# A graph layer with a mixer and experts on one core: TensorE signals by drains, a ring of 16, one ScalarE scaling instead of two, and norm weights folded ahead

## The reference, cut to what matters

```
xn = layernorm(x)
hconv(x, W, b):  xt = x @ W
                 m   = segment_sum(xt[src], dst) / (edges of the dst)
                 out = segment_sum(m[dst], src) / (edges of the src)
                 return out + b
h = prelu(hconv(xn, W1, b1), a);  h = prelu(hconv(h, W2, b2) + xn, a)
x = x + h + mix(xn)          # linear attention: k, v normed per head, dots = sum k v, out = q dots / n
x = x + ffn(layernorm(x))    # its own norm, gamma, beta; top 2 of 8 experts, 256 -> 512 -> 256, gelu
```

## Time and profile before

| | |
|---|---|
| median of 3 runs | 8475.15 us (8469.13 to 8481.79) |
| the profiled execution | 8563.98 us, its span 8562.2 us |
| mean granted TensorE clock in it | 0.743 of full speed |
| PE, DVE, POOL, ACT busy | 55%, 44%, 48%, 16% |

### The profile page before, as it was taken

The page is one execution under the profiler, slowest core; times in us unless marked ns, Lnnn a source line. Parts: engine busy times, 40 slices in busy tenths (PEclk is TensorE's granted clock), DMA queues, the critical chain, the costliest instruction groups (busy, mean ns, idle before and its releaser), DMA issues. The chain is left out here.

```text
span 8562.2 us, 93336 instructions
## 1 busy us (share of the span) xinstructions
PE 4688.6 (55%) x16858; PEld 2911.1 (34%) x16859; DVE 3784.0 (44%) x11251; ACT 1385.0 (16%) x4213; POOL 4105.5 (48%) x4256
## 2 busy tenths in 40 slices
PE   3116976666666645555554455445444544454796
PEld 1014533333333323333332233333223322334564
DVE  5105754444444444444444444444433433367323
ACT  0004843333333300000000000000000000000242
POOL 4761034444444445555555465566565556532342
PEclk7558988888788767787776677777666666666898
DMA  2002011222222142222223333333532222231114
GB/s 85 0 21 72 0 43 58 59 59 59 59 59 59 57 103 78 77 81 80 79 76 76 102 107 108 108 108 110 121 121 83 82 82 83 83 74 51 33 62 130
DMA packets 330997, 639.22 MB, mean 75 GB/s; under 512 B 81808, under 2 KB 201444, under 8 KB 330448
## 3 DMA queue, kind: packets, MB, share of 16 engines
q0 software_dynamic: 191808, 490.67, 21.1%
q1 hardware_dynamic: 131396, 140.16, 5.0%
q10 hardware_dynamic: 7756, 7.97, 0.3%
HBM read 551.49 MB, written 87.01 MB: 75 GB/s over the span
## 5 line engine op out<-in xcount | busy, mean ns | idle before, releaser
L525 POOL DMA_INDIRECT gbuf<-table,idxb x3520 | 3354.6, 953 | 3058.3 <-ACT idxb L650 1351.3
L1342 PE MATMUL PS<-gbuf,ohg 128*128 128x257 f32 x7040 | 2549.8, 494 | 2923.0 <-DVE acc L940 1543.0
L1342 PEld LDWEIGHTS PS<-gbuf,ohg 128*128 128x128 f32 x7040 | 1572.3, 242 | 3818.4 <-DVE acc L940 2000.4
L940 DVE TENSOR_TENSOR acc<-acc,PS 128x257 f32 x3520 | 1498.0, 426 | 2999.0 <-remote 1290.7
L949 DVE TENSOR_SCALAR ohg<-iota,dl 128x128 f32<-128x128 f16 x2664 | 796.0, 305 | 519.9 <-issue 499.9
L1311 PE MATMUL PS<-region 128*128 128x440 f16 x3328 | 851.6, 383 | 0.0
L650 ACT COPY idxb<-idx 128x4 int32 (+1 forms) x884 | 168.0, 190 | 3690.7 <-DVE acc L940 2775.5
L640 ACT ACTIVATE region<-region,acc 128x128 f16<-128x128 f16 x838 | 336.4, 401 | 1300.4 <-DVE region L891 1139.6
L1311 PEld LDWEIGHTS PS<-region 128*128 128x128 f16 x3328 | 355.3, 107 | 337.7 <-issue 100.5
L534 POOL DMA_INDIRECT scattered_d<-acc x384 | 370.2, 964 | 142.7 <-issue 120.2
L890 DVE TENSOR_SCALAR region<-iota_c,acc 128x880 f16<-128x880 f16 x838 | 394.4, 471 | 53.1 <-issue 53.1
(11 more groups left out here) (282 smaller groups left out, 3791.9 us busy)
## 6 DMA issues: line engine op xcount, KB each, us to landing
gbuf<-table,idxb POOLq DMA_INDIRECT x3520
table<-acc SPq DMA_DIRECT2D x21, 896.0 KB, 6.7
region<-xt_d SPq DMA_DIRECT2D x98, 128.0 KB
gbuf<-ye_d SPq DMA_DIRECT2D x12, 1024.0 KB, 7.8
xpad_d<-acc SPq DMA_DIRECT2D x1, 6272.0 KB, 21.8
xn_d<-acc SPq DMA_DIRECT2D x49, 128.0 KB
xt_d<-acc SPq DMA_DIRECT2D x49, 128.0 KB
table<-acc SPq DMA_DIRECT2D x49, 128.0 KB
```

Source lines behind the costliest of these rows:

```text
L525: gp.indirect_dma_start(gbuf[:, k, 0:F], None, tables[p], bass.IndirectOffsetOnAxis(idxb[:, k:k + 1], 0)).then_inc(s_g[k], 16)
L940: TT(a, a, PS[:, 4 + k % AB, 0:FC], ALU.add).then_inc(s_acc[p], 1)
L1342: m = MM(PS[:, 4 + k % AB, 0:FC], ohg[:, k, :], gbuf[:, k, :], start=True, stop=True)
```

## The change

- **Signals.** PE's increments in both histograms (now after every second block), in both ranks, in sort 0 (`s_used`, each fourth column) and in all four passes (`s_mm`) come after a drain. Passes 0 and 1 keep groups of two chunks and four banks; passes 2 and 3 signal after four chunks, use eight half banks and products 256 wide. In pass 0 the two sort columns of a group stand behind its signal; in the other passes `body` stands before the signal.
- **Rank 1 and first norm.** The loop is written out. One drain in each block covers its transposes, its rank matmuls and the product of the block before; SP and ACT wait on finer semaphores, and SP's settling is gone.
- **Sorts.** RING is 16, LEAD (how far the blocks' numbers are read ahead) 8. `ohs` is gone: DVE's compare multiplies by field 1 plus 1 and writes `ohv` directly, and ACT scales that once by (field 2 part) / (field 1 plus 1). For this `fields` gets a reciprocal and a product over 832 columns, and `unpack` a subtraction.
- **Leaky unit of pass 1.** Seven fused operations of 256 columns for a group of seven blocks (times the inverse count, plus bias), ACT makes the negative and the positive part, and one fused operation joins them.
- **Prelude of the experts.** Gamma and beta are folded into W1, Wr, b1 and br during turns 16 to 24 of pass 3. The second norm follows from the variance of the first; POOL's `scale_shift` is gone, ACT normalizes, loads are double.

```
-    AB = 4
-    GP = 2
-    RING = 8
+    RING = 16
+    def banked(p):
+        return 4 if p < 2 else 8
+    def group(p):
+        return 2 if p < 2 else 4
...
-        TS(ohs[o][:, k % RING, :], iota_h[:, :], slot_of[o][:, ds(c, 1)], None, ALU.is_equal).then_inc(s_oh[o], 1)
+        TS(ohv[:, k % RING, 0, :], iota_h[:, :], slot_of[o][:, ds(c, 1)], field_a[o][:, ds(c, 1)],
+           ALU.is_equal, ALU.mult).then_inc(s_oh[o], 1)
...
-        A(ohv[:, k % RING, 0, :], ohs[o][:, k % RING, :], ACT.Copy, scale=field_a[o][:, ds(c, 1)])
-        A(ohv[:, k % RING, 1, :], ohs[o][:, k % RING, :], ACT.Copy, scale=field_b[o][:, ds(c, 1)]).then_inc(s_ohs[o], 1)
+        A(ohv[:, k % RING, 1, :], ohv[:, k % RING, 0, :], ACT.Copy, scale=field_b[o][:, ds(c, 1)]).then_inc(s_ohs[o], 1)
...
-                m.then_inc(s_hist, 1)
+                if b % 2 or b == NB - 1:
+                    signal(s_hist)
...
                 if o == 0 and k % SG == SG - 1:
-                    m.then_inc(s_used, 1)
+                    signal(s_used)
...
-                        if k % GP == 0:
-                            pe.wait_ge(s_acc[p], i * U + (U + k + GP - AB))
-                        m = MM(PS[:, 4 + k % AB, 0:FC], ohg[:, k, :], gbuf[:, k, :], start=True, stop=True)
-                        if k % GP == GP - 1:
-                            m.then_inc(s_mm[p], 1)
+                        if k % group(p) == 0:
+                            pe.wait_ge(s_acc[p], i * U + (U + k + group(p) - banked(p)))
+                        MM(chunk_sum(p, k), ohg[:, k, :], gbuf[:, k, 0:width(p)], start=True, stop=True)
                         if body is not None:
                             body(i, k)
+                        if k % group(p) == group(p) - 1:
+                            signal(s_mm[p])
+                            if columns:
+                                for c in range(k + 1 - group(p), k + 1):
+                                    sort_column(1, i, c)
...
+                link(V.reciprocal(pos, field_a[o][:, 0:EC]))
+                link(TT(field_b[o][:, 0:EC], field_b[o][:, 0:EC], pos, ALU.mult))
...
+                link(TS(a, a, 1, 0, ALU.subtract, ALU.max))
...
+            def fold_body(i, k):
+                if k == 4:
+                    pe.wait_ge(s_shift, i - FOLD + 3)
+                    for kt in range(KT):
+                        m = MM(PS[:, 0, :], fa_["shift"][:, kt, :], fr["w1"][:, ds(i - FOLD, 1), kt, :].rearrange("p a h -> p (a h)"),
+                               start=kt == 0, stop=kt == KT - 1)
+                    signal(s_fold)
...
-                link(norm(lambda j: accs[1][:, ds(q * G + j, 1), 0:F].rearrange("p a f -> p (a f)"), lambda j: low[:, j, :], s_v1, s_d1, q, n))
-                norm(lambda j: low[:, j, :], lambda j: low[:, j, :], s_v2, s_d2, q, n).then_inc(s_xh, 1)
```

More of the change, by code:

```diff
@@ L92, in gps_layer @@
     G = 4
+    FOLD = 16
     ER = 4
@@ L548, in _ @@
                 pool.wait_ge(s_sc[h], SC_TURNS * U * 16)
-            pool.wait_ge(s_lnfree, NR7 + 1)
+            for n in range(3):
+                pool.wait_ge(s_lnd[n], NR7 * PART[n] * 48)
             pool.wait_ge(s_wd, 32)
@@ L703, in _, with fold_gamma @@
             idx_pass(2, 0, TURNS)
-            idx_pass(3, 0, TURNS)
+            def fold_gamma(i, k):
+                if k == 12:
+                    act.wait_ge(s_fold, i - FOLD + 2)
+                    settle(act)
+                    for kt in range(KT):
+                        w = fr["w1"][:, ds(i - FOLD, 1), kt, :].rearrange("p a h -> p (a h)")
+                        A(w, w, ACT.Copy, scale=fr["gb"][:, 0, kt:kt + 1])
+            idx_pass(3, 0, FOLD)
+            act.wait_ge(s_fold, 1)
+            for kt in range(KT):
+                A(fr["wr"][:, kt, :], fr["wr"][:, kt, :], ACT.Copy, scale=fr["gb"][:, 0, kt:kt + 1])
+            idx_pass(3, FOLD, FOLD + NE, fold_gamma)
+            idx_pass(3, FOLD + NE, TURNS)
             def act_first(q, par, n):
@@ L1053, in _, with fold_beta @@
             dve.wait_ge(s_zero, 5)
-            acc_pass(3, 0, TURNS)
+            def fold_beta(i, k):
+                if k == 8:
+                    dve.wait_ge(s_fold, i - FOLD + 2)
+                    b = fa_["b1r"][:, ds(i - FOLD, 1), :].rearrange("p a h -> p (a h)")
+                    TT(b, b, PS[:, 0, :], ALU.add).then_inc(s_shift, 1)
+            acc_pass(3, 0, FOLD)
+            dve.wait_ge(s_fw, N_FW)
+            for kt in range(KT):
+                m = TS(fa_["shift"][:, kt, :], ones[:, :], fr["gb"][:, 1, kt:kt + 1], None, ALU.mult)
+            m.then_inc(s_shift, 1)
+            TS(sm["nega"], a_col[:, 0:1], -1.0, None, ALU.mult).then_inc(s_shift, 1)
+            dve.wait_ge(s_fold, 1)
+            TT(fr["br"], fr["br"], PS[:, 1, 0:NE], ALU.add).then_inc(s_shift, 1)
+            acc_pass(3, FOLD, FOLD + NE, fold_beta)
+            acc_pass(3, FOLD + NE, TURNS)
             dve.wait_ge(s_acc[3], NC + U)
@@ L1265, in _ @@
                 rank(0, b)
+                signal(s_rank)
             pe.wait_ge(s_put, NB)
@@ L1327, in _, with product_pass @@
             close_sort(0)
-            def product_pass(p, start, end, body=None):
+            def product_pass(p, start, end, body=None, columns=False):
                 if start == 0:
@@ L1448, in pe_third @@
                 m.then_inc(s_lg, 1)
-            by_group(pe, pe_first, pe_second, pe_third)
+            for q in range(2):
+                turn_sums(q, G)
+                second_weights(q, q, G)
+            for q in range(1, NG - 1):
+                turn_sums(q + 1, G)
+                turn_rows(q - 1, (q - 1) % 2, G)
+                second_weights(q + 1, (q + 1) % 2, G)
+                logits(q - 1, G)
+            turn_sums(NG, 1)
+            turn_rows(NG - 2, 0, G)
+            second_weights(NG, 0, 1)
+            logits(NG - 2, G)
+            turn_rows(NG - 1, 1, G)
+            logits(NG - 1, G)
+            turn_rows(NG, 0, 1)
+            logits(NG, 1)
             pe.wait_ge(s_ecnt, 1)
```

303 lines of the change are left out of this document (165 added, 138 removed).

## The result

The changed kernel takes 8732.67 us (median of 4 runs, 8730.18 to 8759.25) where the kernel before takes 8478.47 (4 runs, 8469.13 to 8496.68): ratio 1.030, 95% interval 1.028 to 1.033. It is slower by 254 us. I had forecast 123 us: the direction was right and the time lies within the range, but the loss is twice the one that I forecast.

The account below looks back on a forecast made before the run. No single bound: no engine is busy for more than 55% of the span. Terms -3 + 52 + 97 + 92 + 0 - 30 - 100 + 15 = +123 us, added to 8475.15, gave 8598 us, 1.4% slower; range 8320 to 8780.

Parts of the forecast that it names:

- the drains of pass 0 ahead of the hole: Pass 0: half of 8 drains a turn fall where PE waits anyway for late signals, so they cost nothing.
- the prelude: Prelude of the experts: DVE bounds it and sheds statistics, normalizations and other work, -100 us, bounds -70 and -120.
- pass 0: Pass 0: four of 8 drains a turn cost PE 0.47 us each over 52 turns, +97 us, bounds 0 to +195.
- the head: Before sort 0: fields, unpack and histogram 0 cost time, rank 1 gains 24 us; together -3, bounds -60 and +40.
- the leaky unit: Leaky unit of pass 1: a group goes from 9.17 to 4.9 us, seven times, -30 us, bounds -15 and -35.
- sort 0: Sort 0: 112 drains at 0.47 us each, since PE has no gap there, +52 us, bounds 0 and +70.
- pass 1: Pass 1: four of 8 drains a turn cost 0.47 us each over 49 turns, +92 us, bounds 0 and +245.
- passes 2 and 3: Passes 2 and 3: drain costs equal the gains from fewer DVE waits and more banks, 0 us, bounds -165 and +198.
- The rival that signals come sooner: Passes: drains bring DVE's adds into the hole if lateness belongs to increments on matmuls; about 8071 us, chance 0.14.
- moves no number: Sort 0 and pass 0: ACT's fused scaling does nothing; already part of the forecast at 0 us, no chance of its own.
- a signal does miss its place as in the rival: Pass 1: a delayed signal misses the hole, +5 instead of +1.9 us a turn, 8750 us, chance 0.12.
- clock: Sort 0: short gaps from drains halve PE's clock, +334 us, 8930 us, chance 0.04.

Follow-up runs that it names:

- The copy first: The changed kernel with ACT's copy of the previous group's transposed rows moved ahead of its work on the next group in the prelude: 8687.13 us, ratio 1.027.

## Why the prediction was right in direction and wrong in size

Two terms failed: the drains of pass 0 ahead of the hole, put at nothing, and the prelude, put at -100 us. The medians lie 131 us above the forecast. By the table's stages, the prelude is 62 us off, pass 0 30, the head 15, the leaky unit 4, sort 0 2, pass 1 -60, and passes 2 and 3 -12. The remaining 88 or so are in the two profiles' places about their medians.

- **"Each turn thus has a hole for the late signals of PE"**: right, and the drains were late as the rows of the old ones said. The rival that signals come sooner is out: DVE's waits only changed their name, and POOL's waits for row numbers in pass 0 did not get shorter (834 us before, 956 after).
- **Sort 0**: right, +52 forecast, +54 measured.
- **Pass 0, the step that failed**: "Half of them, by the pattern of the earlier trace rows, lie in the rush and half ahead of the hole, where PE waits anyway: 4 × 0.47 = 1.9 us". The drains ahead of the hole were costed at nothing, since PE waits there anyhow. But it waited, in most turns, only after it had used its free banks up to chunk 9; a drain makes it stop at the first late completion. The run without drains prices this: 3.5 us a turn for the stops where I had 0, and 1.3 for the four drains of the rush where I had 1.9, together 4.7 to 4.8 us a turn and 246 us over the pass, above the upper bound of 195 that I had given. In the kernel before the same drains cost 136 us, with the 86 us above open. The stage grew by 127 where +97 was forecast. That it comes that near is partly luck: without its drains the changed kernel needs 113 us less than before (1873 against 1986, the latter from the long profile), a term that I had put at 0 ("hidden", "moves no number"), and with its drains nothing of that is left.
- **Pass 1**: +92 forecast, +32 measured, 17 of it by the drains in the changed kernel; in the kernel before they cost 54. The hole now comes before chunk 4 in 48 turns, where it came before chunk 6 in 46, so a signal does miss its place as in the rival, but the turn grows by 0.5 us and not by 5. That PE has slack behind its hole there is my reading and not tried.
- **Passes 2 and 3**: 0 forecast, and 15 for the fold; +3 measured. Two terms lie under it: the drains cost 52 us, and something else gives them back, which was not separated.
- **Leaky unit**: right, -26 where -30 was forecast; the timeline after has 4.8 us a group where 4.9 was forecast.
- **Prelude, mis-sized**: -100 forecast, -38 measured. "DVE is busy for 217 of 272 us, and bounds it" held only before the change. With DVE's work down from 217 to 129 us the limit became ACT's order, which holds back the logits. The copy first gave 59 of the missing 62 us.
- **Head**: -3 forecast, +12: rank 1 ended 6 us later, since histogram 0 took 6 us more and the scatter ended 13 us later, and fields 1 took 6 us more.
- **"A difference of 100 us taken from it is wrong by about 1 us"**: wrong. It treats the 88.8 us by which the profiled execution lay above the runs as a scale factor. The kernel before spreads by as much: its runs beside the later kernels on late chips took 8435 to 8561 us. If these us lie in the passes, as the kernel before with drains makes likely, the passes together grew by up to 250 us where I had summed 204 with the fold.
- The **clock** did not halve in sort 0: granted at 0.99 over 390 us, with gaps of 0.21 us behind each 16 matmuls, as this timeline of PE in the changed kernel shows. The Trainium skill (TensorE: Matmul & The Clock Gate, "A second HAM failure mode: psum-queue depth-cycling") warns of such short idles; this stage does not bear it out.

```profile
801.52 3.14 PE L1368 MATMUL PS<-acc,region 128*128 128x440 f16 x16 [0.21 <-issue]
804.88 3.14 PE L1368 MATMUL PS<-acc,region 128*128 128x440 f16 x16 [0.21 <-issue]
```

## What to carry to other kernels

A drain is not free where its engine is about to wait: it takes away the work that the engine would still have done in that time. Where signals between engines may come late, let the matmul carry the increment, so that the engine can use the free banks behind it; here that was worth 402 us, 4.6%, against some 1.4% where signals came in time (0.993 and 0.994 against 1.0005, an estimate that adds two runs on different chips). Whether more free banks would help pass 0 was not tried. When an engine is relieved, look for what stands next in order on the engines that feed it, before the gain is booked.

## What the runs showed of the hardware

- The same kernel took 8470 to 8530 us on some chips and 6367 to 6369 on others, with the same work. The difference is when PE's completions reach the other engines while POOL issues indirect transfers: on late chips DVE waited up to 15.1 us for one, on prompt ones its waits carry no such name. Where POOL issues few or none of them in a row, the time is the same on both: 86 and 86 us in the leaky unit, 973 and 974 from the end of pass 3. What sets a chip apart was not found.
- On a late chip a rest of about 1.55 us of POOL ahead of every four indirect transfers made the lateness in the passes vanish (pass 0 from turns of 34.2 to 27.5 us). On a prompt chip it cost its own length.
- A drain on a late chip lasted up to 28.5 us on PE's sequencer (median 2.3), and PE's next matmul and the engine that waited for the signal started together, within 0.04 us; on a prompt chip none lasted over 6.2.
